# First attention with two iterations in flight, its norm's root on GpSimd, split weight load, shared query rotation and another order of the gate products

## The reference

```python
h = tokens                                         # (128, 64, 64)
# L0 attention, on layernorm(h)
q, k, v = x @ Wq + bq, x @ Wk + bk, x @ Wv + bv
a = softmax(q @ k.T / 64) @ v                      # within each image's 64 tokens
y = relu(batchnorm(a @ Wl + bl))                   # statistics over all 8192 tokens
h = h + x + y
# L0 ffn: causal attention with rotary q and k (4 heads of 16), then 2 of 8 SwiGLU experts
q = q * cos + rotate_half(q) * sin ;  k = k * cos + rotate_half(k) * sin
# L1 attention: relative bias, softmax * scale, @ proj, layernorm with gain g2 and bias b2
# L1 ffn: H = gelu(x @ W1 + b1); probs = softmax(H @ Wg); the one expert with the largest
y = sum_e where(e == argmax(probs), probs[e] * (H @ Wd[e] + bd[e]), 0)
```

## Time and profile before

| | |
|---|---|
| median of 3 runs | 8839.58 us (8835.07 to 8847.66) |
| profiled execution | 8844.81 us, of which the span of its instructions is 8843.0 us |
| tokenizer | from the start to about 5854 us |
| loop of l0a | 5875.7 to 6074.4 us, 8 iterations |
| second loop | from 6098.5 us, 8 iterations |
| busy share of the span | PE 83%, DVE 65%, ACT 25%, GpSimd under 1% |

### The profile page before, as it was taken

The page is one execution under the profiler, slowest core; times in us unless marked ns, Lnnn a source line. Parts: engine busy times, 40 slices in busy tenths (PEclk is TensorE's granted clock), DMA queues, the critical chain, the costliest instruction groups (busy, mean ns, idle before and its releaser), DMA issues. The chain is left out here.

```text
span 8843.0 us, 127696 instructions
## 1 busy us (share of the span) xinstructions
PE 7317.0 (83%) x40310; PEld 3642.9 (41%) x40310; DVE 5728.9 (65%) x11559; ACT 2224.5 (25%) x3750; POOL 31.1 (0%) x35
## 2 busy tenths in 40 slices
PE   6888886999999699999879999965666766767667
PEld 5544444544444644444452222223333333333333
DVE  4799995688888478888747777755454454454453
ACT  3222122211111211111132222223333333333333
POOL 0000000000000000000000000000000000000000
PEclk8999998999999899999989999976777777778788
DMA  7655557666666866666684444420000000000000
GB/s 214 136 126 121 126 126 182 193 178 180 181 181 181 219 170 181 181 180 179 169 218 118 122 123 118 117 83 5 1 2 3 1 3 3 1 3 3 1 3 2
DMA packets 641754, 957.80 MB, mean 108 GB/s; under 512 B 527640, under 2 KB 531296, under 8 KB 582758
## 3 DMA queue, kind: packets, MB, share of 16 engines
q1 hardware_dynamic: 641416, 953.52, 40.8%
HBM read 621.97 MB, written 344.28 MB: 109 GB/s over the span
## 5 line engine op out<-in xcount | busy, mean ns | idle before, releaser
L603 PE MATMUL abank<-inv_basis,mode_tile 128*128 128x512 f32 x2048 | 1023.9, 624 | 172.6 <-DMA mode_tile<-m_modes 161.8
L970 DVE TENSOR_TENSOR work<-inv_copy,abank 128x512 f32<-128x512 f32 x1024 | 657.2, 683 | 613.9 <-ACT inv_copy L845 613.5
L665 PEld LDWEIGHTS gbank<-fwd_basis,turned 128*128 128x128 f32 x6368 | 747.1, 193 | 369.8 <-issue 221.5
L665 PE MATMUL gbank<-fwd_basis,turned 128*128 128x128 f32 x6368 | 823.0, 283 | 51.3 <-ACT turned L853 51.3
L1001 DVE TENSOR_TENSOR arena<-zbank,work 128x512 f32<-128x512 f32 x1024 | 701.6, 685 | 207.5 <-PE zbank L638 207.4
L634 PE MATMUL zbank<-arena,conv_bd 128*64 128x512 f32 x3072 | 829.2, 618 | 3.1 <-DVE mixed L1159 2.2
L636 PE MATMUL zbank<-arena,conv_bd 128*64 128x504 f32 x3072 | 779.6, 586 | 0.0
L638 PE MATMUL zbank<-arena,conv_bd 128*64 128x504 f32 x3072 | 779.6, 586 | 0.0
L1003 DVE SCALAR_TENSOR_TENSOR arena<-arena 128x512 f32<-128x512 f32 x1024 | 708.5, 692 | 35.4
L853 ACT ACTIVATE turned<-tbank 128x512 f32<-128x512 f32 x796 | 432.0, 594 | 1100.5 <-PE tbank L652 1100.5
L603 PEld LDWEIGHTS abank<-inv_basis,mode_tile 128*128 128x128 f32 x2048 | 365.4, 196 | 543.6 <-issue 495.4
(11 more groups left out here) (302 smaller groups left out, 9180.3 us busy)
## 6 DMA issues: line engine op xcount, KB each, us to landing
h_rows<-arena SPq DMA_DIRECT2D x192, 1024.0 KB, 16.3
arena<-h_rows SPq DMA_DIRECT2D x192, 1024.0 KB, 6.2
arena<-h_rows SPq DMA_DIRECT2D x384, 496.0 KB, 8.9
m_modes<-mixed SPq DMA_DIRECT2D x64, 1024.0 KB, 6.7
mode_tile<-m_modes SPq DMA_DIRECT2D x512, 128.0 KB, 4.3
g_modes<-modes_out SPq DMA_DIRECT2D x192, 256.0 KB
arena<-x_slots SPq DMA_DIRECT2D x192, 194.9 KB
arena<-g_modes SPq DMA_DIRECT2D x36, 1024.0 KB, 11.0
```

What stands on the lines that cost most here:

```text
L603: last = nc.tensor.matmul(abank[px][:], mode_tile[u][:, 2 * px + k, :, :].rearrange("p a c -> p (a c)"), inv[:, 2 * px + k, :], start=True ...
L665: last = nc.tensor.matmul(gbank[u][:, 128 * k:128 * k + 128], turned[q][:, k // 2, k % 2, b, :], fwd[:, 2 * q + b, k, :], start=(q == 0 an ...
L970: nc.vector.tensor_tensor(inverse[:, 2 * k + part, :], inv_copy[k][:], abank[1][:], op)\
```

## The change

Five edits, besides renamed arguments:

1. Loading: constants first, then the first 517 columns of the weights (all that l0a uses), the token tiles of two iterations, and the other 12120 columns with a semaphore `rest` of their own, which the engines wait for after the l0a loop. The weights are 128 columns narrower.
2. l0a handles two of the old iterations as groups g = 0 and 1 in one loop of ITERS // 2 = 4, step by step in turn, with buffers of its own for each group (`h` and `r`, `x` and `sq`, `small` and `small_b`, the two halves of the PSUM banks). `x.root` on ACT and `x.rstd` on DVE are gone; DVE adds 1e-5 to the variances (`x.vars`, 128x4 each) and GpSimd raises them to -0.5 (`rstd`, 128x2x4, one per group). Both ACT table switches of an iteration go with the root.
3. l0f: a head's 16 q features and 16 rotated ones stand side by side in one 32-row block, so one projection gives both, one DVE product with a table `cossin` makes q, and the scores contract over 32 rows against k held twice.
4. l1a: the softmax scale moves from a DVE step (`scaled`) into ACT's copy of `pT`; the addition of b2 to h (`h_b`) moves from the end of the stage to before `k`.
5. l1f: `y3` stands ahead of `share0`; shares alternate between banks 0 and 1, the sum has bank 2; each share is issued one step ahead of the sum before it. The logits' matmuls alternate between units.

```diff
@@ l0a: the stage functions are new; here PE, ACT, GpSimd
-            stacked_tensor(p, "x", "x.out")
-            attn_tensor(p, "l0a")
+            for g in R:
+                for u in R:
+                    p.need("dve", f"x.out{g}", u)
...
+                p.done_both(last)
+            for g in R:
+                p.need("act", f"xT{g}", 1)
+                p.done_both(mm(B[g][1][:], W("l0a_q"), g_xT[g]))
+            for g in R:
+                p.done_both(mm(B[g][2][:], W("l0a_k"), g_xT[g]))
...
-            table_scalar(ACT.Sqrt)
-            root_scalar(a, "x")
-            table_scalar(ACT.Exp)
...
+        def l0a_pool(p):
+            for g in R:
+                p.need("dve", f"x.vars{g}", 1)
+                p.done_both(nc.gpsimd.tensor_tensor(g_st[g][:, :, 8:12], g_st[g][:, :, 0:4],
+                                                    bmid(W("mhalf")[:, 0:4], U), ALU.pow))
@@ l0a_vector, the order of its steps
+('l0a', 'dve'): IN_TWO(['x.stats', 'x.aggr', 'x.vars', 'x.centered', 'x.out', 'k', 'v', 'max', 'diff', 'sum', 'recip',
+                         'p', 'hx', 'hl']),
@@ l0f
-            for name, b in (("q", 0), ("k", 2)):
...
+            for u in R:
+                p.need("act", "r.xT", u)
+                for n, part in HALVES:
+                    last = mm(B[u][n][:, 0:256], W("l0f_q")[part, :], x2(u)[part, :])
+                p.done(last, "q", u)
...
-                        rows = slice(32 * g, 32 * g + 16)
+                        rows = slice(32 * g, 32 * g + 32)
...
+                d.done(V.tensor_tensor(four(two(Q[u][:])), four(two_banks(u, 0, 0)), table("cossin"), ALU.mult), "q", u)
@@ l1a
+            a.done_both(nc.scalar.activation(a_pT.rearrange("p t n -> p (t n)"), B[1][2][:], ACT.Identity, scale=weight))
-                d.done_both(V.tensor_scalar(a_s, a_s, W(scale), None, ALU.mult))
@@ l1f, after gates_tensor
-            p.need("dve", "gT", 1)
-            share_tensor(p, 0, f_gT)
-            expert_tensor(3)
-            for k in range(1, 3):
-                for u in R:
-                    p.need("dve", f"kept{k - 1}", u)
-                share_tensor(p, k, f_gT)
...
+            expert_tensor(3)
+            p.need("dve", "gT", 1)
+            share_tensor(p, 0, f_gT, 0)
...
+            share_tensor(p, 1, f_gT, 1)
...
+            sum_tensor(p, 0, f_kept, B[0][2])
+            for k in range(2, 4):
+                share_tensor(p, k, f_gT, k - 2)
+                sum_tensor(p, k - 1, f_kept, B[0][2])
+            sum_tensor(p, 3, f_kept, B[0][2])
@@ queues
-            sp.dma_start(wts[:], weights_dram).then_inc(loaded, 16)
             sp.dma_start(cst[:], consts_dram).then_inc(loaded, 16)
+            sp.dma_start(wts[:, 0:first], weights_dram[:, 0:first]).then_inc(loaded, 16)
...
+            sp.dma_start(wts[:, first:], weights_dram[:, first:]).then_inc(rest, 16)
```

More of the change, by code:

```diff
@@ L1372 @@
                  + [f'silu{j}' for j in range(NTILE)] + ['yT'],
[L1373 to L1374 removed]
+ ('l0f', 'dve'): [*TWICE, 'x.rstd', 'x.out', 'q', 'ka', 'kb', 'k', 'masked0', 'masked1', 'masked2', 'masked3', 'max', 'diff', 'sum', 'recip', 'p',
                   'pT1', 'oT1', 'x2', 'f.sumsq', 'f.rstd', 'f.out', 'emax', 'ediff', 'esum', 'erecip', 'probs',
@@ L1381 @@
  ('l1a', 'act'): ['x.root2', 'x.xT', 'q', 'exp', 'pT', 'oT', 'o.root'],
- ('l1a', 'dve'): [*TWICE, 'k', 'v', 'biased', 'max', 'diff', 'sum', 'recip', 'scaled', 'p', 'proj', *NORM('o'),
-                  'o.g', 'h_b', 'h'],
+ ('l1a', 'dve'): [*TWICE, 'h_b', 'k', 'v', 'biased', 'max', 'diff', 'sum', 'recip', 'p', 'proj', *NORM('o'),
+                  'o.g', 'h'],
  ('l1a', 'pe'): ['x.flip', 'q', 'k', 'v', 'scores', 'pT', 'attended', 'proj'],
@@ L1387 @@
                   'chosen', 'gates', 'gT', 'kept0', 'kept1', 'kept2', 'kept3', 'h'],
- ('l1f', 'pe'): ['x.flip', 'hid0', 'hid1', 'logits', 'y0', 'logitsT', 'y1', 'y2', 'gatesT', 'share0', 'y3', 'share1',
-                 'share2', 'sum0', 'sum1', 'share3', 'sum2', 'sum3', 'y'],
+ ('l1f', 'pe'): ['x.flip', 'hid0', 'hid1', 'logits', 'y0', 'logitsT', 'y1', 'y2', 'gatesT', 'y3', 'share0', 'share1',
+                 'sum0', 'share2', 'sum1', 'share3', 'sum2', 'sum3', 'y'],
  ('l2a', 'act'): ['x.root2', 'x.root', 'x.xT', 'hid0', 'qk', 'kexp', 'exp', 'v', 'k4', 'q4T', 'o0', 'f.root', 'f.xT', 'ff0', 'ff1', 'yT'],
@@ L1794, in l0a_vector @@
-        def l0a_vector(d):
[L1795 to L1804, removed]
+        pick = lambda a, b: (a, b)
@@ L2105, in l1a_vector @@
             scaled_vector(d, "x", "x.rstd2", r, x_of, again, "r.out")
-            attn_vector(d, "l1a", rel="l1a_rel", scale="l1a_scale")
+            for u in R:
+                d.done(V.tensor_tensor(h[u][:], h[u][:], bmid(W("l1a_b2"), T), ALU.add), "h_b", u)
+            attn_vector(d, "l1a", rel="l1a_rel")
             for u in R:
@@ L2144, in sum_tensor @@
             for u in R:
-                p.done(mm(B[0][1][rows[u], :], W("fold"), kept(u, k), start=(k == 0), stop=(k == 3)), f"sum{k}", u)
+                p.done(mm(bank[rows[u], :], W("fold"), kept(u, k), start=(k == 0), stop=(k == 3)), f"sum{k}", u)
         def expert_scalar(a, k, bank, bias, kept):
@@ L2817, in _ @@
             pool.wait_ge(loaded, 32)
+            with pool.Fori(0, ITERS // 2) as it:
+                l0a_pool(Engine(sig, "pool", pool, "l0a", it))
             pool.wait_ge(bn_done["dve"], 4)
```

299 lines of the change are left out of this document (204 added, 95 removed).

## The result

The changed kernel takes 8688.47 us (median of 4 runs, 8682.11 to 8698.72) against 8843.62 for the kernel before on the same chip (4 runs, 8835.07 to 8850.27): a ratio of 0.9828, 95% interval 0.9813 to 0.9842, 155 us faster. The four runs spread over 17 us. The profiled execution, the fastest of them, took 8682.11 us with a span of 8680.3; the profiled one of before had a span of 8843.0, so the two traces differ by 162.7 us.

A forecast was written before the change was run, and what follows sets the result against it. No engine is full in l0a: single chains of waits after an idle load; the second loop mixes dense stretches and chains. 14 + 55 + 14.7 + 7.2 + 43 = 134 gives 8711, or 8706 against the median; range 8676 to 8762.

The forecast's parts named there:

- The load, 14.0: Loading before l0a: the wait of 21.75 us falls to 7.8, gain 14.0 us, bounds 12 and 16.
- l0a, 55: l0a loop: overlapping two groups saves 50 us in four pairs, the clock 4.5 more; gain taken as 55 us.
- nothing on the path: l0a's power on GpSimd: about 1 us each, hidden up to 1.15 each behind DVE's centering and PE's flips.
- the dear rival: GpSimd's power in l0a takes 3.7 us each, a pair 5.2 longer, 21 in all; total 8727; chance 0.12.
- The once-only load of 6 us: GpSimd's first call: a skill rule's instruction-memory load of about 6 us, lowering the sum once; taken as nothing by the trace.
- At full clock the late k and all v take half: l0a's PE work: 3 us less per pair possible; a third taken, 1.1 per pair, 4.5 in all, bounds 0 and 12.
- the layout: l0a's pair of groups laid out with the single chain's durations: period 37.1 us against 49.7, 12.6 saved per pair.
- l0f, 1.84 per iteration: l0f, first projection to scores: 10.04 us becomes 8.2, gain 14.7 in all; bounds 1.2 and 2.7 (k at full clock).
- l1a, 0.9: l1a: `scaled` leaves the chain and `h_b` falls into DVE's wait for k; gain 0.9 us per iteration, 7.2 in eight.
- l1f, 5.4: l1f, gates' copy to `yT`: from 19.20 us to 12.8 or 15.3; gain 5.4 taken, 43 in all, bounds 0.7 and 6.4.
- A fall earlier than the forecast's: Rival: the clock falls early in l1f, gain 0.7 instead of 5.4 us per iteration; total 8744; chance 0.09.
- 8690, full clock in both places: Rival: l1f gains 6.4 us per iteration and l0a's clock 12 instead of 4.5; total 8690; chance 0.07.

The follow-up runs named there:

- the two runs that took it away: Changed kernel with l0a's root on ACT and reciprocal on DVE: 8688.7 us; with group 0's statistics, aggregation and variances ahead of group 1's on DVE: 8679.1 us.
- The run without overlap: Changed kernel with each engine taking group 0's whole l0a chain, then group 1's, power and split load kept: 8759.9 us (ratio 0.9911).
- two neighbouring kernels: Changed kernel with l0f's old query rotation: 8723.6 us; changed kernel with 40 and 44 unread transposes filling PE's waits in l0a: 8734.1 us.
- The kernel with ACT's root: Changed kernel with the root of l0a's variance on ACT and the reciprocal on DVE instead of GpSimd's power: 8688.7 us (ratio 0.9834).
- the kernel with early variances: Changed kernel with group 0's statistics, aggregation and variances ahead of group 1's on DVE in l0a: 8679.1 us (ratio 0.9823).
- the two kernels: Changed kernel with l1f's old order, three full matmuls in kept1's wait: 8726.9 us; with l0f's old rotation, two in l1f's kept0 wait: 8678.3 us.
- two kernels with the same rows of PE ahead of it: The changed kernel, 8688.47 us, and the changed kernel with l0f's query rotation as before, l1f new, 8723.6 us.

## Why the prediction came out as it did

The forecast was 8706 with 134 us gained; 155 were measured, and 162.7 between the traces, of which 3.85 lie in the tokenizer, which no edit touches. 8688.5 lies in the range but 3.5 us outside the forecast's own 8692 to 8722. The signs of all five terms held, and their mechanisms too but for the power, which was put at nothing on the path. The sizes erred mostly on the same side.

**The load, 14.0.** Measured 14.95; the range was 12 to 16. The rest of the weights cost nothing to be seen. No run undid this edit alone, so this stands on the two traces.

**l0a, 55.** Measured 61.8, and two errors met in it. "I take about 1 us, nothing on the path" was wrong for the power: 1.64 alone and 2.83 for the first of each pair, 2.0 to 2.3 us per pair on the path by the two runs that took it away (8.2 and 9.1 in four). The place was the one named as what would make the forecast wrong ("if DVE waits for GpSimd before `x.out`"), at less than half the price of the dear rival. The once-only load of 6 us that the prediction weighed did not show: the program's first power took 2.83 us, as did the first of each later pair. "At full clock the late k and all v take half ... I take a third, 1.1 per pair" was wrong the other way. From the flips (5864.42) to the first `max` (5874.94) the layout had 12.9 us and the trace has 10.5, since k and v run at full clock; `hl`, costed at 1.97 per group, took 1.08 and 1.05, and the end from its start on shrank from 5.45 to 3.8. With 0.5 between `max` and `hl` that is 4.5 per pair instead of 1.1. The layout itself held: 37.1 at the low clock, less 4.5, plus 1.7 for the first power gives 34.3, and 34.1 to 34.3 were measured. The loop thus came out at 136.9 and not at the 144 to 150 named as a sign. The run without overlap showed that the overlap carries the clock with it: the loop is 71.8 longer and PE's busy time back at 91.

**l0f, 1.84 per iteration.** First projection to scores shrank by 2.00 in the second iteration, about as laid out. The stage's mean fell by 3.2 (98.2 to 95.0): in that iteration 2.0 ahead of the scores and 1.0 from their start to the end of the stage; in the four of the shorter kind 2.8 ahead of them, the case of the upper bound (k at full clock). The scores' own row is the same over 32 rows as over 16 (1.88 and 1.90 us), as costed. What was not in the sum: with the old rotation l1f loses its clock in six of eight iterations, so undoing the edit cost 35 us and not 15.

**l1a, 0.9.** Measured 0.8, from the traces alone.

**l1f, 5.4.** Measured 6.1; undoing it cost 5.9 per iteration of the total. "At full clock `yT` starts at 12.8" came out at 12.9 in every iteration, which is the case of full clock that had a chance of 0.07, not the value between two cases that the forecast took. The argument for it (PE works more densely, as in the expert loop) does not carry it alone: the same dense order lost its clock in eleven of sixteen iterations of two neighbouring kernels. That it held in all eight here was in part luck. A fall earlier than the forecast's, put at 0.09, happens in those kernels: 5.7 us after the copy, with 17.6 us from copy to `yT`. The logits' new order gave nothing, as forecast.

The rival "8690, full clock in both places" came closest, and for the reason given there in l1f; in l0a the clock gave a gain of that kind, but the power took half of it back.

## What to carry to other kernels

An operation moved to another engine has to be placed by when its operand is ready, not only priced: the same power cost some 2 us per pair behind both groups' statistics and next to nothing behind the first group's. Two chains in flight gain twice, by the filled waits and by the clock that the denser work keeps, so the rows of a single chain at the low clock overstate the joined one. Where the clock is near to falling, an edit is worth what it does to the whole iteration: undo one edit and look at the granted clock of stages that it doesn't touch, and fill a wait on PE where a fall starts before shortening anything else.

## What the runs showed that was not expected

**Lengths of an iteration.** In all fourteen kernels the seven intervals between gates' copies were 331.1, 334.5, 337.9, 341.3 (341.6 in the kernel before) or 344.6 us, within 0.4, whatever had been cut or added inside: l0f 3 us longer, two full matmuls more, y3 moved. A gain or loss inside a stage of the second loop shows in these executions only as a change from one of these lengths to another. The kernel with ACT's root shows it in its own trace: 9.1 us less in l0a, and from the end of that loop on 2699.5 us against 2686.5, which is what four intervals of 334.5 in place of 331.1 make. What ties them to these lengths was not tried.

**The power beside DVE.** Alone it took 1.64 us for 128x8 and 0.54 for 64x1. It took 2.83 when it began 0.10 us behind DVE's first subtraction, and ended 1.5 after the last of them; begun 0.23 behind it, in the kernel with early variances, it took 1.68 beside the same operations. The Trainium skill, SBUF — State Buffer, section "SBUF: two separate sides", says that a DVE operation with two inputs in SBUF and a GpSimd operation that reads SBUF lock one pair of ports against each other for the whole instruction, and that the one that starts first has it. The first of these rows agrees with that, the second does not. Nor does the second power of each pair: it starts 0.14 us ahead of DVE's multiplications (5863.37 and 5863.51), and both take their usual time, 1.63 and 0.76 for two. No run here settles what tells them apart.

**The clock and waits.** The Trainium skill, TensorE: Matmul & The Clock Gate, section "HAM oscillation", has it that idle gaps between bursts lose the clock; its example has longer ones than these. The filled waits agree: no fall ahead of `yT` in sixteen iterations of the two kernels, where without the full matmuls fourteen of sixteen had one. But two kernels with the same rows of PE ahead of it, down to the 0.70 us wait, differed in whether it fell, so from one stage's rows alone it can't be read.
